# A gated cross-attention and feed-forward block: attention work dealt out anew among the engines, x2 without its row constant, a feed-forward that begins and ends in halves

## The reference

```
query = ctx @ Wq.T + bq                 # the same context for both
key   = ctx @ Wk.T + bk
attention = softmax(query @ key.T)      # 256 x 256 for each batch
x = x + tanh(g_xattn) * (layernorm(x) @ attention.T)
h = layernorm(x).astype(e4m3)
a = (gelu(h @ w_gating[0]) * (h @ w_gating[1])).astype(e4m3)   # 1024 hidden
x = x + tanh(g_ffn) * (a @ w_linear)
```

## Time and profile before

| | |
|---|---|
| runs | 51.0, 50.4, 50.01 us; median 50.4 |
| profiled execution | 49.82 us, span 48.0 |
| PE busy | 42.2 us, 88% of the span |
| DVE busy | 35.5 us, 74% |
| ACT busy | 29.4 us, 61% |
| POOL busy | 16.9 us, 35% |

### The profile page before, as it was taken

How to read it: one execution, slowest core, us unless ns; L and a number is a source line. 1 busy time by engine, 2 the same in 40 slices (tenths; PEclk the granted TensorE clock), 3 DMA queues, 4 the chain that set the end, 5 groups by cost and what they waited for, 6 DMA issues and landing times.

```text
span 48.0 us, 844 instructions
## 1 busy us (share of the span) xinstructions
PE 42.2 (88%) x246; PEld 28.9 (60%) x246; DVE 35.5 (74%) x110; ACT 29.4 (61%) x67; POOL 16.9 (35%) x35
## 2 busy tenths in 40 slices
PE   3999999985999999998999999999999999994300
PEld 1318788845788888853446655565657688862000
DVE  0103649999797979799999981987666998899900
ACT  0641866597996999464797959744448943572000
POOL 3200899059899360600700430000000895006000
PEclk9999999999999999999999999999999999999965
DMA  0399799999999950000000000000000035300092
GB/s 0 50 367 369 282 391 400 301 174 155 106 104 105 103 46 0 0 7 14 0 0 0 0 0 0 0 7 0 0 0 0 0 123 190 122 16 0 0 338 99
DMA packets 3605, 4.64 MB, mean 97 GB/s; under 512 B 401, under 2 KB 2321, under 8 KB 3601
## 3 DMA queue, kind: packets, MB, share of 16 engines
q1 hardware_dynamic: 2448, 3.61, 22.1%
q0 software_dynamic: 864, 0.79, 17.6%
q10 hardware_dynamic: 288, 0.20, 1.3%
HBM read 5.90 MB, written 1.05 MB: 145 GB/s over the span
## 4 chain that ended last, share of the span: by engine, by line
PE 65%; DVE 13%; DMA 9%; SPq 3%; ACT 2%; issue 1%; DVEq 1%
PE bank L638 15%; PE bank L644 14%; PE bank L663 14%; PE bank L598 14%; DMA x_sb<-x 9%; DVE st L413 4%; PE bank L570 4%; DVE nmax L420 2%; PE bank L620 2%; PE bank L563 2%; SPq L208 2%; DVE aq L480 2%; DVE mv L416 1%; DVE attn L431 1%; ACT xq L347 1%
## 5 line engine op out<-in xcount | busy, mean ns | idle before, releaser
L471 DVE SCALAR_TENSOR_TENSOR ap<-bank,gl 128x512 f16<-128x512 f32 (+1 forms) x20 | 11.6, 581 | 3.5 <-issue 1.6
L356 ACT ACTIVATE gl<-bank 128x512 bf16<-128x512 f32 (+1 forms) x20 | 10.0, 508 | 6.0 <-PE bank L638 6.0
L663 PE MATMUL bank<-wl,aq 128*128 128x256 fp8e4 x64 | 10.1, 273 | 0.7 <-DVE aq L480 0.6
L638 PE MATMUL bank<-xq,wg 128*128 128x512 fp8e4 (+1 forms) x40 | 10.2, 337 | 0.2 <-ACT xq L347 0.2
L644 PE MATMUL bank<-xq,wg 128*128 128x512 fp8e4 (+1 forms) x40 | 10.2, 337 | 0.0
L663 PEld LDWEIGHTS bank<-wl,aq 128*128 128x128 f16 x64 | 6.0, 98 | 4.1 <-DVE aq L480 1.6
L598 PE MATMUL bank<-attnT,xT_sb 128*128 128x256 f32 x32 | 8.1, 385 | 0.0
L480 DVE TENSOR_SCALAR aq<-ap 128x512 uint16<-128x512 uint16 (+1 forms) x20 | 6.6, 334 | 0.0
L277 POOL TENSOR_TENSOR yo<-ys,x 128x256 f32<-128x256 f32 x4 | 2.9, 746 | 9.3 <-ACT ys L364 9.3
L598 PEld LDWEIGHTS bank<-attnT,xT_sb 128*128 128x128 f32 x32 | 5.6, 190 | 0.7 <-ACT attnT L330 0.2
L262 POOL TENSOR_TENSOR r<-ve,neg_half 128x2 f32<-128x2 f32 x4 | 3.0, 758 | 8.5 <-DVE ve L454 8.5
(11 more groups left out here) (50 smaller groups left out, 54.4 us busy)
## 6 DMA issues: line engine op xcount, KB each, us to landing
x_sb<-x SPq DMA_DIRECT2D x4, 256.0 KB, 4.6
xT_sb<-xT SPq DMA_DIRECT2D x4, 256.0 KB, 5.7
out<-yo SPq DMA_DIRECT2D x6, 128.0 KB, 2.1
wg<-w_gating POOLq DMA_DIRECT2D x4, 128.0 KB, 8.4
par<-params_ctxT SPq DMA_DIRECT2D x1, 256.0 KB, 4.3
wl<-w_linear POOLq DMA_DIRECT2D x2, 128.0 KB, 8.4
out<-yo SPq DMA_DIRECT2D x1, 256.0 KB, 2.0
par<-params_ctxT SPq DMA_DIRECT2D x1, 192.0 KB, 2.8
```

The costliest lines, as they stand in the source:

```text
L356: nc.scalar.activation(gl[:, s % 2, toks], gate_b[s % 2][:, toks], ACT.Gelu_apprx_tanh).then_inc(gelu_ready, 1)
L471: nc.vector.scalar_tensor_tensor(ap[:, s % NAP, toks], up_b[s % 2][:, toks], ACT_SCALE, gl[:, s % 2, toks], ALU.mult, ALU.mult).then_inc(p ...
L638: mm = nc.tensor.matmul(gate_b[s % 2][:, toks], wg8[:, c, k, 0, o:o + P], xq[:, g, k, toks], start=(k == 0), stop=(k == KC - 1))
L663: mm = nc.tensor.matmul(halves(y_b[g][i])[:, t], aq[:, s % NAQ, m:m + P], wl8[:, j], start=(j == 0 and t == 0), stop=(j == HT - 1), skip_g ...
```

## The change

1. k_out moves from ACT to DVE. 2. The scaling of the exponentials for all four batches is POOL's. 3. scales1 is made per pair of batches, and yields only s1; the row constant nms1 is made later (shifts1), since x2 is now x + s1 * pv without it. The second layer norm doesn't see a constant of the row, so only the output needs it: it comes in as the bias of ACT's scale_out, or for three halves through a copy x2s that ACT makes in feed-forward steps 8 to 10. 4. stats1 is spread along DVE's stream; turn_attention and turn_x2 wait half by half. 5. PE's stream interleaves anew: turn_x2(0) stands before the second half of attend(2). 6. The first hidden block of the first pair is worked in halves (FIRST = 1), ffn1(0) stands before turn_x2(1), and SPLIT falls from 4 to 3. The steps are again 20. 7. Two ffn2 at the end are held back (HOLD = 2). 8. POOL's last addition waits for the last rounding.

```diff
-    SPLIT = 4
-    STEPS = [divmod(n, HT) + (0, GB) for n in range(G * HT - SPLIT)]
+    SPLIT = 3
+    HOLD = 2
+    FIRST = 1
+    STEPS = [(0, j, i, i + 1) for i in range(GB) for j in range(FIRST)]
+    STEPS += [divmod(n, HT) + (0, GB) for n in range(FIRST, G * HT - SPLIT)]
     STEPS += [(G - 1, j, i, i + 1) for i in range(GB) for j in range(HT - SPLIT, HT)]
-    X_AFTER = (3, 6)
+    X_AFTER = (4, 7)
...
# POOL
+            def scales1(h):
+                pair = slice(h * B // 2, (h + 1) * B // 2)
+                pool.wait_ge(mv1_ready, LT * (h + 1) * B // 2)
+                nc.gpsimd.tensor_scalar(ve1[:, pair], mv1[:, pair, :, 1], EPS, None, ALU.add).then_inc(ve1_ready, 1)
+                pool.wait_ge(ve1_ready, h + 1)
+                nc.gpsimd.tensor_tensor(r1[:, pair], ve1[:, pair], neg_half[:, pair], ALU.pow).then_inc(r1_ready, 1)
...
+                nc.gpsimd.tensor_scalar(s1[:, pair], r1[:, pair], tg[:, 0:1], None, ALU.mult).then_inc(s1_ready, 1)
...
-            scales1()
-            shift_x(0)
-            shift_x(1)
-            normalise(B - 1)
+            normalise(0)
+            normalise(1)
+            scales1(0)
+            normalise(2)
+            normalise(3)
+            scales1(1)
             for b in range(B):
                 rstd2(b)
+                if b == 1:
+                    shifts1()
             for k in range(LT * GB):
                 add_residual(k)
-            pool.wait_ge(scaled_ready, GB + 1)
+            pool.wait_ge(aq_ready, S)
+            pool.wait_ge(scaled_ready, LT * GB + 1)
...
# ACT
             q_out(0)
-            k_out(0)
             q_out(1)
-            k_out(1)
             q_out(2)
-            k_out(2)
             exps(0)
             q_out(3)
-            k_out(3)
             exps(1)
             attn_out(0)
             exps(2)
+            attn_out(1)
             exps(3)
-            attn_out(1)
             attn_out(2)
             nc.scalar.activation(table[:, :], tg[:, 0:1], ACT.Gelu_apprx_tanh)
-            shift_x(2)
             attn_out(3)
-            shift_x(3)
             xq_out(0)
-            xq_out(1)
             for s in range(S):
                 gelu(s)
+                if s == FIRST - 1:
+                    xq_out(1)
...
# DVE
+            def k_out(b):
+                dve.wait_ge(k_done, b + 1)
+                nc.vector.tensor_scalar(kT[:, b * L:(b + 1) * L], k_b[b % 2][:, 0:L], bk, None,
+                                        ALU.add).then_inc(k_ready, 1)
...
-            for b in range(B - 1):
-                stats1(b)
+            k_out(0)
+            stats1(0)
+            k_out(1)
             row_max(0)
-            stats1(B - 1)
+            k_out(2)
+            stats1(1)
             row_max(1)
-            normalise(0)
+            invert_sum(0)
+            k_out(3)
             row_max(2)
-            normalise(1)
+            invert_sum(1)
             row_max(3)
-            normalise(2)
-            invert_sum(B - 1)
-            for b in range(2):
-                add_attention(b)
-                stats2(b, 0)
-                stats2(b, 1)
-                moments2(b)
+            stats1(2)
+            invert_sum(2)
+            add_attention(0)
+            invert_sum(3)
+            stats2(0, 0)
+            stats2(0, 1)
+            moments2(0)
+            stats1(3)
+            add_attention(1)
+            stats2(1, 0)
+            stats2(1, 1)
+            moments2(1)
             norm2(0)
+            add_attention(2)
             norm2(1)
-            add_attention(2)
             stats2(2, 0)
             stats2(2, 1)
             moments2(2)
...
# PE
             attend(0, [(0, 0), (0, 1)])
             turn_attention(1)
             attend(0, [(1, 0), (1, 1)])
+            attend(1, [(0, 0), (0, 1)])
             turn_attention(2)
-            attend(1)
+            attend(1, [(1, 0), (1, 1)])
             turn_attention(3)
-            attend(2)
+            attend(2, [(0, 0), (0, 1)])
+            turn_x2(0)
+            attend(2, [(1, 0), (1, 1)])
             attend(3, [(0, 0), (0, 1)])
-            turn_x2(0)
-            attend(3, [(1, 0)])
+            ffn1(0)
             turn_x2(1)
-            attend(3, [(1, 1)])
+            attend(3, [(1, 0), (1, 1)])
             for s in range(S):
-                ffn1(s)
-                if s >= LAG:
+                if s > 0:
+                    ffn1(s)
+                if LAG <= s < S - HOLD:
                     ffn2(s - LAG)
...
-            for s in range(S - LAG, S):
+            for s in range(S - LAG - HOLD, S):
                 ffn2(s)
```

More of the change, by code:

```diff
@@ L108, in flamingo_block @@
         nms1 = sb("nms1", [P, B, LT], F32)
[L109 removed]
+        x2s = sb("x2s", [P, LT + 1, D], F32)
         x2 = sb("x2", [P, B, LT, D], F32)
@@ L196, in flamingo_block @@
         s_out = sem("s_out")
+        first_of_g1 = next(s for s, step in enumerate(STEPS) if step[0] == 1)
         def last_step(b):
@@ L238, in load_w_gating, with shifts1 @@
                 pool.dma_start(wg8[:, c], w_gating[c]).then_inc(s_wg[c], 16)
[L240 to L254, removed]
+            def scales1(h):
[4 more added lines that the diff above has]
+                nc.gpsimd.tensor_tensor(r1[:, pair], ve1[:, pair], neg_half[:, pair], ALU.pow).then_inc(r1_ready, 1)
+                pool.wait_ge(r1_ready, h + 1)
+                if h == 0:
+                    pool.wait_ge(ntg_ready, 1)
+                nc.gpsimd.tensor_scalar(s1[:, pair], r1[:, pair], tg[:, 0:1], None, ALU.mult).then_inc(s1_ready, 1)
+            def shifts1():
                 nc.gpsimd.tensor_scalar(nr1[:, :, :], r1[:, :, :], ntg[:, 0:1], None, ALU.mult).then_inc(nr1_ready, 1)
-                nc.gpsimd.tensor_scalar(s1[:, :, :], r1[:, :, :], tg[:, 0:1], None, ALU.mult).then_inc(s1_ready, 1)
                 pool.wait_ge(nr1_ready, 1)
@@ L330, in attn_out, with shift_x2 @@
                 nc.scalar.copy(attnT[:, b].rearrange("p k d -> p (k d)"), turn_b[b % 2][:, :]).then_inc(attnT_ready, 1)
[L332 to L336, removed]
+            def shift_x2(n):
+                b, t = ((2, 0), (3, 0), (3, 1))[n]
+                if n == 0:
+                    act.wait_ge(nms1_ready, 1)
+                act.wait_ge(x2_ready, LT * b + t + 1)
+                nc.scalar.activation(x2s[:, n], x2[:, b, t], ACT.Identity,
+                                     bias=nms1[:, b, t:t + 1]).then_inc(x2s_ready, 1)
             def norm2(b):
@@ L398, in _ @@
                     xq_out(3)
[L399 to L406, removed]
+                if X_AFTER[1] < s <= X_AFTER[1] + LT + 1:
+                    shift_x2(s - X_AFTER[1] - 1)
+                if s == first_of_g1 + LAG:
+                    scale_out(0, 0)
+                    scale_out(0, 1)
+                if s == first_of_g1 + LAG + 1:
+                    scale_out(1, 0)
+                    scale_out(1, 1)
+            scale_out(2, 1)
         @block.vector
@@ L529, in _ @@
             round_product(S - 1)
[L531 to L534, removed]
+            dve.wait_ge(scaled_ready, LT * GB + 1)
+            finish(0)
+            finish(1)
+            finish(2)
         @block.tensor
@@ L565, in energy @@
                 mm.then_inc(energy_done, 1)
[L567 to L572, removed]
             def turn_attention(b):
@@ L586, in turn_attention @@
                     pe.wait_ge(q_ready, B)
-                turn(turn_b[b % 2], attn[:, b]).then_inc(attn_turned, 1)
+                for t in range(LT):
+                    pe.wait_ge(pool_attn_ready, LT * b + t + 1)
+                    for k in range(KC):
+                        mm = nc.tensor.transpose(halves(turn_b[b % 2])[:, k, t * P:(t + 1) * P],
+                                                 attn[:, b, t, k * P:(k + 1) * P], ident[:, :])
+                mm.then_inc(attn_turned, 1)
             def attend(b, parts=tuple(pairs(range(LT), range(KC)))):
@@ L616, in turn_x2 @@
                     pe.wait_ge(ident8_ready, 1)
-                for k in range(KC):
-                    for t in range(LT):
+                for t in range(LT):
+                    if b < 2:
+                        pe.wait_ge(xh_ready, LT * b + t + 1)
+                    else:
+                        pe.wait_ge(act_xh_ready, LT * (b - 2) + t + 1)
+                    for k in range(KC):
                         mm = nc.tensor.matmul(halves(x2_b[b])[:, k, t * P:(t + 1) * P],
```

53 lines of the change are left out of this document (16 added, 37 removed).

## The result

The changed kernel took 53.62 us (median of four, 52.98 to 53.86) against 50.59 for the kernel before: ratio 1.060, 95% interval 1.034 to 1.086, slower. Medians are over all executions of a set, while the ratios compare only executions in the faster of two states that the executions of any kernel fall into, so a ratio isn't quite the quotient of the medians. The forecast was 52.6 in 50.3 to 54.3, by the stop of PE that the profile now shows. The profiled executions stand 4.0 apart, 53.86 to 49.82 (spans 52.1 and 48.0); the one profiled in the second set took 53.51.

The account below looks back on a forecast made before the run. PE was taken to bound the kernel, with a new stop at turn_x2(0) for POOL's late r2(0). Feed-forward +2.7, stall -0.17 and end -0.3 gave +2.2 on 50.4: 52.6 us, range 50.3 to 54.3.

Parts of the forecast that it names:

- The stop: At turn_x2(0), PE waits from 17.84 to 20.65 for xh(0), behind POOL's late r2(0): 2.8 us.
- How late: Feed-forward start: after three groups PE stands at 26.2, before at 23.48, so 2.7 us late.
- The chance of 0.1 for the clock: Rival, behind PE's stop: the granted clock falls to the lower level, +1.7 to +3.5, 54.3 to 56 us; chance 0.1.
- The total: Whole kernel: +2.7 - 0.17 - 0.3 = +2.2 us, on the median 50.4 giving 52.6.
- the mild end of the clock's fall: Lower end of the clock's 54.3 to 56 us after PE's stop: 54.3, taken as the range's upper end.
- With one more full step there I count that stall gone: Feed-forward with SPLIT 3: the ffn2 taking 0.61 instead of 0.44 goes away, -0.17 us (0 to -0.17).
- The end: Last rounding 0.22 instead of 0.70 as POOL waits; -0.3 of the 0.48 us (-0.1 to -0.5); HOLD 0.
- The hold-up by edit 2: At moments2(0), POOL's scaling of batch 3 would delay DVE's ve by up to 0.47 us; nothing taken in the sum.
- PE meets no wait: Rival, at turn_x2(0): xh(0) is there by 17.84, feed-forward 1.1 to 1.3 early, 48.7 us; chance 0.13.
- nothing is lost: Rival, whole kernel: the stop is there, but PE's earlier arrival and the end pay for it; chance 0.05.
- DVE bounds, not POOL: Rival, at norm2(0): r2(0) is there when DVE comes at 19.4, 0.8 less, 51.2 to 51.8 us; chance 0.22.

Follow-up runs that it names:

- the second set: The changed kernel run once more, nothing altered, against the kernel before: 53.51 us against 50.24, ratio 1.072.
- e2: Changed kernel with 11 matmuls on constants ahead of turn_x2(0), where PE stops: 52.93 us, ratio 1.050 to the kernel before.
- e7: HOLD = 0 in the changed kernel with rstd2(0), norm2(0) and statistics moved early: 50.38 us, ratio 1.010 to the kernel before.
- e6: POOL's wait for the last rounding deleted in the changed kernel with rstd2(0), norm2(0) and statistics moved early: 50.45 us, ratio 1.011 to the kernel before.
- e3: Changed kernel with POOL's rstd2(0) ahead of scales1(1), nothing else moved: 51.93 us, ratio 1.039 to the kernel before.
- e9: Kernel before with only turn_x2(0) moved between the halves of attend(2): 51.61 us, ratio 1.022 to the kernel before.

## Why the prediction was right, and where its terms were off

- **The stop.** PE came to the turn at 18.46, not 17.84: POOL took up its first scaling at 10.37, not 10.06, as the reciprocal was later than counted and 0.2 lay between them, and energy(3) began at 11.64 for 11.25. xh(0) came at 20.9, not 20.6. The stop was 2.51, for 2.8. Of the 0.7 that the attention stage was to gain by then, 0.2 came: energy(3) began at 11.64, before at 11.80. The sum from DVE's last statistics to r2(0), 2.55, measured 17.92 to 20.38, 2.46, with the power at 1.04 for an interpolated 1.05. k_out costs 0.40 in DVE's queue (8.18 to 8.58), the upper row, for 0.35.
- **How late.** I forecast 2.7 us at the third group. By the order alone that is about right in size: e2, at full clock, has a rest 3.0 above before's, from which the end's gain of 0.2 has been taken already. The chance of 0.1 for the clock was the weak step. The third block's up matmuls were to begin at 26.2 and began at 27.62, 1.4 later, and the eight attends alone took 1.4 more than in e2 (3.17 against 1.78, by the start of what follows). The clock fell in both profiled executions, after a stop shorter than I had forecast. Its price was 0.9 to 1.2, below my 1.7 to 3.5, because the low level held until 24.2 and caught little but those eight attends, where I had put 3.5 us of work under it, and because the waits behind them took part of it up.
- **The total.** The loss was to be 2.2 us. By the medians it was 3.0 and 3.3, between the two profiled executions 4.0. That 53.62 still lies in the range is in part luck: the upper end was the forecast with the mild end of the clock's fall on top, and a fall to which I gave one chance in ten did come, but below the lowest price that I had put on it. The direction and the stop that it rests on were no luck.
- **"With one more full step there I count that stall gone"**: wrong, the 0.61 is there again at 43.88. Worth 0.17.
- **The end**: from the gate of the last step but one to SP's last issue it is 45.86 to 50.21, 4.35, against 41.63 to 46.17, 4.54 before: -0.19, for -0.3. HOLD at nothing was right by e7, where POOL's wait stands. But giving POOL's wait the whole credit wasn't: by e6 it does nothing beside HOLD. The Trainium skill's page "SBUF — State Buffer", section "Who interferes with whom", says that DVE in its two-port modes and GpSimd block each other for a whole instruction; that fits a rounding of 0.70 with the addition beside it and 0.23 without. The hold-up by edit 2 that I derived from the rule didn't come: DVE's ve of moments2(0) ran from 16.80 to 16.97, beside POOL's scaling, which lasted until 16.92, and took 0.17, as before.
- **Rivals.** "PE meets no wait" and "nothing is lost" fell with the first row. "DVE bounds, not POOL" is e3's case, a smaller stop: POOL was late, but with POOL prompt DVE's order alone held PE for 1.70. I had put them as alternatives; they stand one behind the other.

## What to carry to other kernels

On an in-order engine, place a short dependent instruction by when its input is ready on the slowest queue before it, and count on each engine what stands in front of its producer: here one 0.2 us turn moved up by eight matmuls cost 1.2 us where POOL's part of its input was early, and 2.6 where it was late, the clock's share included. When such a stop grows, read the granted clock behind it: here the last 0.8 us of a stop cost 2.0. And when an edit undone by itself changes nothing, it may be because another edit already avoids the same collision; only undoing both tells what they are worth.

## What the runs showed of the hardware

PE idle for 2.51 us came back at a granted clock of 0.50, for 3.3 to 3.4 us of work, in both profiles of the changed kernel; idle for 1.70 (e3) or 1.39 (e9) it came back at 1.00. Eleven matmuls on constants in the stop, writing a bank that is overwritten, held the clock at 1.00 in e2's profile. POOL's power cost 0.69 to 0.83 us for 128x2, 1.04 for 128x4 and 1.67 for 128x8. DVE's rounding of 128x256 took 0.21 to 0.23 alone and 0.70 beside POOL's addition.
